# ScalarE at the seam of two stages: the comparison's function loaded early, the second normalising copies behind two comparisons, the turned tiles copied ahead, a lead of 4 tiles

## The reference, cut to what matters

```python
def _L1_gnn_ref(x, adj, W, a, gamma, beta):
    ...
    h_prime = jnp.einsum('ijh,jhd->ihd', attn, Wh).reshape(n, H * D)
    mean = jnp.mean(h_prime, axis=0)
    var = jnp.var(h_prime, axis=0)
    h_prime = gamma * (h_prime - mean) * jax.lax.rsqrt(var + EPS) + beta
    return jax.nn.relu(h_prime)

def _L2_gnn_ref(X, A, W_nb, b_nb, W_line, b_line, neibor_num):
    Ab = A > 0
    keep = Ab & (jnp.cumsum(Ab.astype(jnp.int32), axis=1) <= neibor_num)
    cnt = keep.sum(axis=1, keepdims=True).astype(X.dtype)
    nb_sum = keep.astype(X.dtype) @ X
    nb_mean = nb_sum / jnp.maximum(cnt, 1.0)
    xj = jax.nn.leaky_relu(nb_mean @ W_nb.T + b_nb)
    xi = jax.nn.leaky_relu(X @ W_line.T + b_line)
    return xi + jnp.where(cnt > 0, xj, jnp.zeros((), X.dtype))
...
    x = _layernorm(x + _L1_gnn_ref(x, adj, ...), axis=-1)
    x = _layernorm(x + _L2_gnn_ref(x, adj, ..., 64), axis=-1)
```

## Time and profile before

| | us |
|---|---|
| device time, median of 3 runs | 866.36 (864.34 to 868.39) |
| the profiled execution's own time | 866.28 |
| its span, first to last instruction | 864.4 |
| PE busy | 813.0 (94%) |
| DVE busy | 665.1 (77%) |
| ACT busy | 574.2 (66%) |
| POOL busy | 132.3 (15%) |

### The profile page before, as it was taken

One profiled execution on the slowest core, in us unless ns is written; L12 is line 12 of the kernel. 1 busy time (PEld: TensorE's weight loads), 2 busy tenths in 40 slices (PEclk: granted clock), 3 DMA queues, 4 the chain that ended last, 5 costly groups with the idle time before them and its releaser, 6 DMA issues. The chain is left out here.

```text
span 864.4 us, 18885 instructions
## 1 busy us (share of the span) xinstructions
PE 813.0 (94%) x7821; PEld 510.5 (59%) x7821; DVE 665.1 (77%) x1037; ACT 574.2 (66%) x577; POOL 132.3 (15%) x287
## 2 busy tenths in 40 slices
PE   3899999999999999997879999999968999999997
PEld 1344444334444444443569999999943557777786
DVE  6686969698898979795899999999852686555444
ACT  6798989897767777773479999999668631111000
POOL 2511011233110010001410000000001352111122
PEclk9999999999999999998979999999989999999999
DMA  8966344395302020002121111110000000000011
GB/s 288 269 197 170 111 142 141 99 212 116 99 12 62 1 61 1 14 1 82 51 77 51 52 52 52 52 51 4 2 2 0 1 1 1 1 2 1 1 50 49
DMA packets 28616, 56.87 MB, mean 66 GB/s; under 512 B 5808, under 2 KB 10032, under 8 KB 27120
## 3 DMA queue, kind: packets, MB, share of 16 engines
q1 hardware_dynamic: 24400, 46.19, 17.9%
q0 software_dynamic: 4128, 9.44, 4.4%
HBM read 38.70 MB, written 2.23 MB: 47 GB/s over the span
## 5 line engine op out<-in xcount | busy, mean ns | idle before, releaser
L489 ACT ACTIVATE ex<-scores_ps,shift 128x1024 f32<-128x1024 f32 x256 | 262.7, 1132 | 59.1 <-PE scores_ps L345 51.5
L563 DVE TENSOR_TENSOR esum<-esum,ex 128x1024 f32<-128x1024 f32 x192 | 223.3, 1219 | 18.1 <-ACT ex L489 17.9
L341 PE MATMUL scores_ps<-qst,kst 128*128 128x512 f32 x512 | 200.7, 473 | 2.9 <-ACT ex L489 2.3
L1020 PE MATMUL banks<-fx,pos 128*128 128x132 f16 x2048 | 162.0, 223 | 5.8 <-DVE pos L1206 5.8
L1299 ACT ACTIVATE steps<-a_all,big_b_head 128x2048 fp8e5<-128x2048 f32 x86 | 163.6, 1990 | 0.0
L345 PE MATMUL scores_ps<-edge,negI 128*128 128x512 fp8e5 x512 | 155.2, 385 | 0.0
L341 PEld LDWEIGHTS scores_ps<-qst,kst 128*128 128x128 f32 x512 | 89.3, 189 | 72.6 <-ACT ex L489 23.0
L1020 PEld LDWEIGHTS banks<-fx,pos 128*128 128x128 fp8e5 x2048 | 122.6, 98 | 6.5 <-issue 5.0
L1027 PE MATMUL banks<-fm,edge 128*128 128x66 f16 x2048 | 104.9, 194 | 0.0
L1027 PEld LDWEIGHTS banks<-fm,edge 128*128 128x128 fp8e5 x2048 | 87.4, 98 | 0.0
L1206 DVE TENSOR_TENSOR pos<-steps,edge 128x1024 int32<-128x1024 int32 (+1 forms) x65 | 77.4, 1202 | 2.4 <-ACT steps L1299 1.3
(11 more groups left out here) (213 smaller groups left out, 878.4 us busy)
## 6 DMA issues: line engine op xcount, KB each, us to landing
adj_raw<-in_adjT_dram SPq DMA_DIRECT2D x32, 512.0 KB, 5.4
a_all<-score_rows_dram SPq DMA_DIRECT2D x7, 1024.0 KB, 4.7
kst<-high_low SPq DMA_DIRECT2D x56, 64.0 KB, 5.2
kst<-high_low POOLq DMA_DIRECT2D x56, 64.0 KB, 5.6
qst<-high_low POOLq DMA_DIRECT2D x56, 64.0 KB, 2.0
qst<-high_low SPq DMA_DIRECT2D x56, 64.0 KB, 3.7
ex<-in_x2T_dram SPq DMA_DIRECT2D x2, 1024.0 KB, 6.9
ex<-in_xT_dram SPq DMA_DIRECT2D x2, 1024.0 KB, 9.0
```

The source lines that it names most:

```text
L341: nc.tensor.matmul(to, kst[:, h, jt * P:(jt + 1) * P], qst[:, it % 2, h, :], start=True, stop=False)
L489: nc.scalar.activation(ex[:, s % ER, h, :], scores_ps[:, u % SR, :], ACT.Exp, bias=shift[:, it // NC * HG + h:it // NC * HG + h + 1], scal ...
L563: nc.vector.tensor_tensor(esum[:, h, :], other, ex[:, s % ER, h, :], ALU.add).then_inc(summed, 1)
L1020: done = nc.tensor.matmul(place(half, i), pos[:, group_of(h, k, half) % GR, jt % GU, i * P:(i + 1) * P], fx[:, e, jt].rearrange("p k r c - ...
```

## The change

Four edits, all in ScalarE's list but for the constant, which TensorE reads too.

```diff
@@ layer1, ScalarE, after the last head's comparisons
                     if last:
                         pair.scale_weights(act)
+                        count.prepare(act)
@@ tail
     TD = 4
-    LEAD = 6
+    LEAD = 4
@@ tail, ScalarE
+                count.prepare(act)
                 for half in range(2):
                     apply(0, half)
                 for t in range(count.AHEAD, LEAD):
                     count.compare(act, cum_ps, t)
                 for half in range(2):
                     apply(1, half)
                 for s in range(T + HIGH):
+                    if 0 <= s - PROJ < T:
+                        keep_turned(0, s - PROJ)
                     if s + LEAD < T:
                         count.compare(act, cum_ps, s + LEAD)
                     if s == T - LEAD + 1:
                         keep_degrees()
-                    if 0 <= s - PROJ < T:
-                        keep_turned(0, s - PROJ)
                     if s >= HIGH:
                         keep_high(0, s - HIGH)
@@ Cumulation
+        self.scrap = S.sb("scrap", [P, 1], fp32)
...
+    def prepare(self, act):
+        act.wait_ge(self.consts, 3)
+        self.nc.scalar.activation(self.scrap[:], self.limit[:], ACT.Sigmoid)
```

## The result

| | before | after |
|---|---|---|
| device time, median of 7 runs each, us | 864.6 (863.57 to 868.39) | 860.68 (859.31 to 863.95) |
| ratio, 95% interval | | 0.9949 [0.9934, 0.9965] |
| the profiled execution's own time | 866.28 | 863.95 |
| its span | 864.4 | 862.1 |

The change makes the kernel faster by 4.4 us (3.0 to 5.7), where 6.3 were forecast. The 4.4 us follow from the ratio; the means, 865.2 and 860.8, are as far apart, the medians 3.9 us. The sign, the range and most of the mechanism held; the size did not.

A forecast was written before the change was run, and what follows sets the result against it. TensorE was taken to set the pace behind the seam, passing gains through; comparison-cumulation hand-overs held the stretch ahead. 2.71 + 0 + 4.60 + 1.35 - 2.40 = 6.26 us; 866.28 - 6.26 = 860.0, range 857.6 to 864.8.

The forecast's parts named there:

- What bounds the kernel: Behind 722 us TensorE is busy with work the change leaves alone, so any seam gain goes through one for one.
- The load at the count: Loading in ScalarE's idle time before tile 0's comparison ends the block 2.71 us sooner; 1.28 if the clock still falls.
- The loads in the tail: Tile 2 is compared 1.28 us earlier, but TensorE's sixteen turns hold tile 3's comparison: worth 0, at most 1.28.
- rival F: TensorE's second set of turns falls at full clock, so the tail's load counts too: 858.7 us, chance 0.05.
- `apply(1, ...)`: In the tail it follows two fewer comparison pairs of 2.30 us, so it and steps 0 to 2 come 4.60 us earlier.
- The factors' margin: At `apply(1, ...)`, its factors are ready 0.66 us ahead, so comparison pairs are what it waits for.
- The turned copy: In step 3, copying ahead of the comparison removes TensorE's 1.40 us wait: 1.35 gained, ends 1.03 and 1.40.
- Given back: From step 4 to VectorE's normalising in step 13, two more steps with a cumulation lose 2.40 us.
- The worst case: Two tiles' TensorE work, 3.48, plus the degrees' copies, 1.91, in full behind step 4: 5.39 us lost.
- rival C: The lead's gain is given back in full behind step 4, 5.39 instead of 2.40: 863.0 us, chance 0.14.
- The rule on the load's price: A skill rule adds a 1.38 us drain per ScalarE load, giving 858.6 us; the prediction left it out.
- rival E: TensorE's clock stays low from the 1.66 us gap until step 5: 11.3 us more, 871.3 us, chance 0.06.

The follow-up runs named there:

- e3: The kernel before with only the early function load at the count added; ratio to before 0.9979, timed 1.8 us faster.
- e5: The kernel before with only the early function load at the tail's start added; ratio to before 1.0000.
- e4: The changed kernel with 11 zero-weight matmuls filling TensorE's gap at the tail's start; ratio to before 0.9920.
- e6: The kernel before with only the turned copy put ahead of the comparison; ratio to before 0.9987, timed 1.1 us faster.
- e1: The changed kernel with the lead put back from 4 to 6 tiles; ratio to before 0.9953.
- e9: The changed kernel with zero-weight matmuls in two TensorE gaps, 11 at the tail's start and 7 behind back(0); ratio to before 0.9916.
- e2: The kernel before with only the lead changed, from 6 to 4 tiles; ratio to before 0.9979, timed 1.8 us faster.
- e11: The kernel of e9 with a lead of 5 tiles instead of 4; ratio to before 0.9925.
- e13: The kernel of e9 with the old lead of 6 tiles instead of 4; ratio to before 0.9938.
- e10: The kernel of e9 with a lead of 3 tiles instead of 4; ratio to before 0.9926.
- e12: The changed kernel, unaltered, run once more for its profile; no timed ratio, seam 88.15 us.

## Why the prediction was right or wrong

The median of 860.68 lies nearer to the forecast 860.0 than the gain does to its 6.3, and that is luck: the sum started from a profiled execution of 866.28, while the median of the seven runs of before is 864.6. The start was 1.7 us too high, and the gain, 3.9 by the medians, 2.3 us too large.

- *What bounds the kernel.* Right. The 143.08 us behind the seam are the same in both profiles, and whatever the seam gained came through.
- *The load at the count, 2.71.* Right in size where the clock falls (2.68, and 2.69 in e3). As a mean over executions it is less: the low clock that makes up 1.4 of it fell in three executions of four. The prediction took the clock of one profile for that of the kernel; its lower end of 1.28 was the worth in the others. Timed alone it gave 1.8 (e3), so in the timed runs up to 0.9 us of what is missing may lie here, which the one pair of profiles below can't show.
- *The loads in the tail, 0.* Right (e5), and the reason too, TensorE's sixteen turns: with these at full clock the comparison of tile 3 moves up by 2.2 us in e4, part of it the load's 1.28. This is rival F's mechanism; it did not come by itself but had to be made.
- *`apply(1, ...)`, 4.60.* Right: 4.61 against the comparison in front of it. The factors' margin was right as well; only at a lead of 3 do they come last.
- *The turned copy, 1.35.* Right: 1.32 in e6, and from step 0 to step 4 it takes 12.60 us in e1 and 12.61 in e6 and e9, against 14.06 before, 1.45 less.
- *Given back, 2.40.* Right: 2.28 after, 2.41 in e2. The worst case and rival C did not come.
- *The rule on the load's price.* The drain of 1.38 us that the Trainium skill adds to a load ("ScalarE: Activation LUTs", "What ACT_TABLE_LOAD costs") did not show: the comparison in e3 gained no more than the 1.28 load and the clock's 1.4, and e6 shows the two apart.
- *The step that failed* is the one that let steps 0 to 2 "run at the 2.30 pace too", and with it "tile 3's comparison stays at 647.66". After the 4.35 us gap TensorE was back at full clock not with the end of its sixteen turns but only about 647.3, so that tile 3's comparison came 0.73 us later behind the load, and behind the 1.66 us gap the clock fell again, which cost 1.46 us up to step 4. A low clock in steps 0 to 5 was the prediction's own sign of being wrong. That gap was held to be harmless because the profile before showed it so. It is rival E's mechanism, which was given 0.06, at a small size: low for some 3 us and not until step 5. 6.26 - 0.73 - 1.46 = 4.07, and 4.27 were measured in the same pair of profiles; the remaining 0.2 is the copy's 0.1 and the give-back's 0.12. That the clock was the cause of the first is shown by e4, e9, e11 and e13, which add work and have tile 3's comparison at 6.00 or 6.01 us, 2.18 sooner. For the second, e9 takes 1.47 us away, and e10, e11 and e13 show no low clock there either; but as the clock does not always fall in that gap, and the time hardly moved, it is shown for the profiles and not for the timed runs. That the timed 4.4 comes so near to the 4.27 of one pair of profiles proves nothing further.

What stays open is how often the clock falls in each gap. Steps 0 to 2 had it in three of four profiles of a lead of 4 with the gap unfilled (after, e12, e4; not e2) and in none of five with a lead of 6. A timed run carries no profile, only its mean granted clock over the whole span, which low stretches elsewhere move too. Of the 55 runs of the kernel before beside the experiments 12 show 0.989 or 0.990 and the others 0.984 to 0.987, and the median of the 12 is 1.6 us lower (863.9 and 865.5); all five of e9 show 0.989 or 0.990, the six of e4 0.986 to 0.992. That fits the account and doesn't settle it. Whether the lead itself makes this gap more dangerous was not separated from chance; that it does so by standing sooner behind a first low stretch is unlikely, as in e4 there was none ahead and the clock fell all the same. Filling the gap at the count was not tried.

## What to carry to other kernels

A one-column activation of the function that comes next hides its load in an idle stretch ahead and costs 0.2 us, but it pays only where the first user is what others wait for. The load's place was worth 1.28 us, the clock behind it as much again: when a stretch with short waits of TensorE is shortened or moved, price it at both clock levels, and read more than one execution before a gap is called harmless. A lead between two engines has a best value where its gain up front (2.30 us a tile here) meets the wait that comes next, and what it gives back (1.2 us a tile) is paid later, in steps where TensorE sets the pace.

## What the runs showed of the hardware that was not expected

The same gap, in the same place of programs that are alike up to there or nearly so, can be followed by the full clock or by the lower one: 2.11 us at the count led to 0.50 in three executions and to 1.00 in one, and the unfilled 1.66 us in step 0 to 0.50 in three executions of nine, all three with a lead of 4. And 11 matmuls of zeros in the gap of 4.35 us, busy for 2.5 us, kept the clock at 1.00 in five profiles of five although 1.63 us of pause stayed, where it fell in eight of eight without them, and made the kernel 2.5 us faster.
